# Moving POOL's four scatters of the routing table behind the mask of the next iteration, and cutting two of its subtractions into pieces

## The reference

```
x = x + xattn(layernorm(x), ctx, mask)
x = x + ffn(layernorm(x))

xattn: q = w8a8(x, wq, bq)            # rows and weights rounded to 8-bit integers
       k = ctx @ wk.T + bk            # ctx: 375 rows of 512 for each sequence, in float32
       v = ctx @ wv.T + bv
       attn = softmax(q k / sqrt(32) + mask)      # 16 heads of 32 channels
       return w8a8(attn v, wo, bo)
ffn:   probs = softmax(h @ router.T)              # 8 experts
       the two best experts of each token, their probabilities scaled to a sum of 1
       out = sum over both of p * (silu(gate) * up) @ down.T      # 352 inner channels
```

## Time and profile before

| What | Value |
|---|---|
| Median of 3 runs | 1654.12 us (1648.59 to 1658.02) |
| Profiled execution, its own time | 1643.64 us |
| Its span | 1641.9 us |
| Granted clock of PE, mean | 0.972 of full speed |
| PE busy | 1505.0 us, 92% of the span |
| DVE busy | 932.9 us, 57% |
| ACT busy | 880.2 us, 54% |
| POOL busy | 710.8 us, 43% |

### The profile page before, as it was taken

The page is one execution under the profiler, slowest core; times in us unless marked ns, Lnnn a source line. Parts: engine busy times, 40 slices in busy tenths (PEclk is TensorE's granted clock), DMA queues, the critical chain, the costliest instruction groups (busy, mean ns, idle before and its releaser), DMA issues. The chain is left out here.

```text
span 1641.9 us, 39981 instructions
## 1 busy us (share of the span) xinstructions
PE 1505.0 (92%) x11561; PEld 1319.5 (80%) x11562; DVE 932.9 (57%) x2531; ACT 880.2 (54%) x2112; POOL 710.8 (43%) x702
## 2 busy tenths in 40 slices
PE   2899999999999999999999999997199999999896
PEld 2788887888878888788887888886199999999895
DVE  6557776867768677686776867765322222222221
ACT  2466666666666666666666666665033333333232
POOL 4233435444354443544435444343345555555452
PEclk9899999999999999999999999997599999999998
DMA  5667776677766776667766677758236776765643
GB/s 197 170 173 207 196 203 180 175 215 178 208 173 179 210 196 190 173 182 206 197 189 173 182 209 189 196 148 267 68 62 163 171 172 143 167 148 115 167 77 46
DMA packets 219152, 281.53 MB, mean 171 GB/s; under 512 B 82081, under 2 KB 163873, under 8 KB 219105
## 3 DMA queue, kind: packets, MB, share of 16 engines
q1 hardware_dynamic: 200928, 247.78, 53.8%
q0 software_dynamic: 18176, 33.17, 11.5%
HBM read 118.12 MB, written 66.77 MB: 113 GB/s over the span
## 5 line engine op out<-in xcount | busy, mean ns | idle before, releaser
L503 ACT ACTIVATE probs<-probs,neg_max 112x375 f32<-112x375 f32 x512 | 311.8, 609 | 238.8 <-DVE neg_max L579 226.4
L579 DVE CUSTOM_DVE_ANT_0 probs<-score,neg_mask 112x375 f32<-112x375 f32 x512 | 279.5, 546 | 200.0 <-PE score L741 178.9
L749 PE MATMUL turn<-ident,probs 112*125 112x112 f32 x1536 | 265.1, 282 | 6.4 <-ACT probs L503 4.9
L749 PEld LDWEIGHTS turn<-ident,probs 112*125 112x125 f32 x1536 | 227.1, 191 | 40.5 <-issue 16.1
L496 ACT ACTIVATE probs_t<-turn 125x336 f32<-125x336 f32 x512 | 225.5, 440 | 56.4 <-PE turn L749 51.7
L741 PE MATMUL score<-k_stack,q_stack 96*112 96x376 f32 x512 | 209.4, 409 | 5.7 <-DMA q_stack<-q_lo 4.0
L777 PE MATMUL proj<-down_hi,gate_up_hi 128*128 128x376 f32 x512 | 175.6, 343 | 7.4 <-DVE gate_up_lo L606 5.7
L991 POOL DMA_INDIRECT out<-y_rows,entries x63 | 102.2, 1622 | 174.8 <-ACT y_rows L1017 138.8
L1029 DVE TENSOR_TENSOR a_lo<-a_ps,a_hi 128x384 fp32r<-128x384 f32 x63 | 35.1, 558 | 245.1 <-ACT a_hi L1004 157.1
L777 PE MATMUL proj<-down_lo,gate_up_hi 128*128 128x376 f32 x512 | 172.2, 336 | 0.0
L777 PE MATMUL proj<-down_hi,gate_up_lo 128*128 128x376 f32 x512 | 172.1, 336 | 0.0
(11 more groups left out here) (196 smaller groups left out, 3515.0 us busy)
## 6 DMA issues: line engine op xcount, KB each, us to landing
k_stack<-gate_up_hi SPq DMA_DIRECT2D x512, 94.0 KB, 2.2
k_stack<-gate_up_lo SPq DMA_DIRECT2D x256, 94.0 KB, 2.2
ctx_stage<-ctx_t SPq DMA_DIRECT2D x32, 750.0 KB
q_stack<-q_hi SPq DMA_DIRECT2D x256, 56.0 KB, 2.0
w_raw<-gate_up_t SPq DMA_DIRECT2D x32, 352.0 KB, 3.1
gate_up_dram_hi<-w_hi SPq DMA_DIRECT2D x32, 352.0 KB
gate_up_dram_lo<-w_raw SPq DMA_DIRECT2D x32, 352.0 KB
gate_up_hi<-gate_up_dram_hi SPq DMA_DIRECT2D x16, 704.0 KB
```

The source lines that it names most:

```text
L503: act.activation(probs[:, h % DS, :], probs[:, h % DS, :], ACT.Exp, bias=neg_max[:, par % 2, h:h + 1], scale=-1.0, accum_out=total[:, par ...
L579: dve.tensor_tensor_reduce(probs[:, h % DS, :], score[h % 2][0:N, 0:L], neg_mask[:, p, :], 1.0, BIG, ALU.add, ALU.min, neg_max[:, p, h:h + ...
L749: mm = pe.transpose(turn[h % 2][0:LC, l * N:(l + 1) * N], probs[:, h % DS, l * LC:(l + 1) * LC], W["ident"][0:N, 0:N])
```

## The change

The four scatters of a pair become a function of their own. It is called in the next even iteration, behind the negated mask L437 and ahead of the bias on q, and once more behind all iterations for the last pair. The two subtractions for the low parts are cut into instructions on one quarter of ctx (376 columns) and one third of the weights' slice (352 columns); the semaphore is raised by the last piece. Nothing that is computed changes.

```
+            def scatter(pair):
+
+                need(pool, weighing, WEIGH * pair + 6)
+                need(pool, routed, ROUTE * pair + 10)
+                waited(pool)
+                for b in range(2):
+                    for i in range(2):
+                        pool.indirect_dma_start(slots, bass.IndirectOffsetOnAxis(ap=at[:, b, i:i + 1], axis=0), entry[:, b, i, :], None).then_inc(entered, 16)
...
                     pool.tensor_scalar(neg_mask[:, q, :], neg_mask[:, q, :], -1.0, 0.0, ALU.mult, ALU.add).then_inc(mask_negated, 1)
+                if has_m2 and par % 2 == 0 and (inside or pair > 0):
+                    scatter(pair - 1)
                 if has_m2 and par % 2:
                     need(pool, top_made, 2 * pair + 2)
...
                     need(pool, c_hi_made, nn + 1)
-                    pool.tensor_tensor(c_lo[:, par % 2, :, :], stage[:, :, :], c_hi[:, par % 2, :, :].bitcast(F32),
-                                       ALU.subtract).then_inc(c_lo_made, 1)
+                    for t in range(KT):
+                        low = pool.tensor_tensor(c_lo[:, par % 2, t, :], stage[:, t, :], c_hi[:, par % 2, t, :].bitcast(F32), ALU.subtract)
+                    low.then_inc(c_lo_made, 1)
                 if has_n:
                     need(pool, w_hi_made, n + 1)
                     need(pool, w_stored, 64 * n)
-                    pool.tensor_tensor(w_lo[:, :], w_raw[:, :], w_hi[:, :].bitcast(F32), ALU.subtract).then_inc(w_lo_made, 1)
+                    for piece in range(3):
+                        cols = slice(piece * (WG + WD) // 3, (piece + 1) * (WG + WD) // 3)
+                        low = pool.tensor_tensor(w_lo[:, cols], w_raw[:, cols], w_hi[:, cols].bitcast(F32), ALU.subtract)
+                    low.then_inc(w_lo_made, 1)
...
-                    need(pool, weighing, WEIGH * pair + 6)
-                    need(pool, routed, ROUTE * pair + 10)
-                    waited(pool)
-                    for b in range(2):
-                        for i in range(2):
-                            pool.indirect_dma_start(slots, bass.IndirectOffsetOnAxis(ap=at[:, b, i:i + 1], axis=0), entry[:, b, i, :], None).then_inc(entered, 16)
 
             iterations(pool, body)
+            scatter(B // 2 - 1)
             pool.wait_ge(entered, 32 * B)
```

## The result

| | Before | Changed |
|---|---|---|
| Median, runs of the comparison | 1656.07 us (1648.59 to 1658.35, 4 runs) | 1691.2 us (1688.41 to 1696.95, 4 runs) |
| Ratio, 95% interval | | 1.0225 (1.0181 to 1.0269) |
| Profiled execution, own time | 1643.64 us | 1692.43 us |
| Its span, mean granted clock | 1641.9 us, 0.972 | 1690.7 us, 0.949 |

What follows compares the result with a forecast made beforehand. TensorE, busy 92% of the span, was taken as the bound. Ring +21.7, tail -1.5 and clock +18 gave +38 us on 1643.6, thus 1682, or 1692 us as median; range 1655 to 1716 us.

Steps and rivals of the forecast that it cites:

- The pause leaves L762: Product of probabilities and values, even iterations: TensorE's 2.27 us loss goes, its 48 matmuls taking 1.36 us.
- The ring grows by 1.55 us a pair: Loop q's split, SP's queue, mask, POOL, q's transpose, TensorE: mask-to-q 7.3 us against 5.74; +21.7 us over 14 pairs.
- rival 3: SP's queue and mask transfer quicken without scatters; mask 1.5 us earlier, ring unchanged, 1652 us; chance 0.10.
- 37.5 us or more: Sign: the way from q's transpose in the odd iteration to the even one, instead of 35.95 us.
- The clock falls in half of the fourteen: TensorE idling before q's transpose lowers its clock in half the even iterations, 2.6 us each: +18 us, ends 0 and 42.
- second rival: Wait for q comes and TensorE's clock falls in all fourteen even iterations: +56 us, 1710 us; chance 0.19.
- The pieces are worth 0: Cut subtractions on POOL: VectorE's L654 starts earlier, but the gain only lengthens idle time before L789; 0 us.
- The other end, -9 us: Best case for the cut subtractions, against the forecast of 0: a gain of 9 us.
- fifth rival: POOL takes the next piece before VectorE; L654 stays at 0.95 us. No time hangs on it; changes no chances.
- The tail, -1.5 us: Iteration 32, without q: of VectorE's 3.04 us wait for L427, about 1.5 us come back.
- I added 10.5 us: Step from profiled execution's forecast, 1682 us, to the median: the earlier runs' median, 1654.1, lay 10.5 us above that execution.

Runs made afterwards that it cites:

- TensorE kept busy: Changed kernel plus fourteen unread matmuls on TensorE ahead of its wait for q in even iterations: 1661.91 us, ratio 1.0061.
- the move alone: Changed kernel with the two subtractions whole again, scatters still moved: 1691.67 us, ratio 1.0236.
- early scatters and whole subtractions: Changed kernel with the scatters ahead of POOL's wait for the mask and both subtractions whole: 1657.22 us, ratio 1.0066.
- the last comparison: ACT's timelines in two changed kernels with scatters ahead of the mask's wait: mask also loaded ahead of keys' copies (1656.93 us) against without that (1619.36 us).
- 1641.87: Changed kernel with the mask's load issued ahead of the second half's keys' copies and both subtractions whole: 1641.87 us, ratio 0.9945.
- 1656.93: Changed kernel with pieces, mask's load ahead of the keys' copies and scatters ahead of the mask's wait: 1656.93 us, ratio 1.004.
- 1664.76: Kernel of 1657.22 us with ACT's and DVE's instructions shifted by 16 unused increments: 1664.76 us, ratio 1.0095.
- 1698.58: Changed kernel with the scatters one place later, behind the bias on q: 1698.58 us, ratio 1.03.
- 1612.1: Changed kernel, scatters and pieces kept, SP issuing the mask's load ahead of the second half's keys' copies: 1612.1 us, ratio 0.9747.
- 1619.36: Changed kernel, pieces kept, with the scatters moved ahead of POOL's wait for the mask: 1619.36 us, ratio 0.9795.

## Why the prediction was right, and where it was not

**The pause leaves L762: right.** The 48 matmuls take 1.36 us.

**The ring grows by 1.55 us a pair: right in its form, wrong in its size.** From the mask's negation to the transpose of q it takes 7.07 us on average, where 7.3 was worked out; the gap ahead of the first scatter is 0.41 us instead of 0.6. My mean for the kernel before, 5.74 us, is drawn down by the first even iteration; the thirteen others have 5.92. And one sentence failed: "Does the mask come earlier once TensorE is faster? It doesn't". The negation begins 25.09 us behind q's first copy instead of 25.67. Of these 0.58 us, 0.17 are SP's issuing and 0.41 the way from the load's issue to the negation. It is rival 3 with over a third of its size. So 7.07 - 5.92 - 0.58 = +0.57 us, and 0.55 were measured. The term was 7.2 + 3.1 = 10.3 us where 21.7 stood, below its own lower end of 17.5. The sign "37.5 us or more" was therefore missed: it was 36.48.

**The clock falls in half of the fourteen: the size right, the number wrong.** Behind a fall the way is 35.06 - 32.32 = 2.74 us longer, where 2.6 were taken; with TensorE kept busy 2.41 of these come back, and the other 0.33 stay without a cause shown. The fall came in thirteen of fourteen, thus 35.6 us instead of 18. Waits of 3.0 to 4.0 us (6.36 in the first) always brought it, and 1.71 us did not. My half was only a middle between a 3.42 us wait that lowered the clock and pauses of 2.27 us that never did; all new waits but one lay within 0.4 us of the former or above it, so the nearer row should have had nearly all the weight. It would be too much to read a limit into these numbers: in the kernel with the move alone 1.72 us were followed by a fall, and among waits of 1.3 to 2.3 us in the kernel with early scatters and whole subtractions five of thirteen were, without the longer ones being singled out.

The thirteen stretches at 0.56 to 0.63 are the loop that the Trainium skill describes in "TensorE: Matmul & The Clock Gate", section "HAM oscillation — how this bites in real kernels"; this trace agrees with it. The second rival was right about the clock, with a ring of half its size.

**The pieces are worth 0: right** in the changed kernel (1.0236 without, 1.0225 with them). The other end, -9 us, had the wrong sign in the kernel before, where they cost 0.6%, most of it in a longer pause. The fifth rival fell: L654's addition takes 499 ns instead of 951.

**The tail, -1.5 us**, can't be told from the 2.9 us that the span lost outside the pairs counted above.

**The sum.** +38 us were worked out, 48.8 came from span to span, and 35.1 between the medians of the comparison, since the profiled execution of before lay 12 us below that median. The two terms that were off went opposite ways, -11 and +18. That the forecast met the median within 1 us owes something to chance. I added 10.5 us because the profiled execution of before lay below its median; that of the changed kernel lies 1.2 us above its own.

## What to carry to other kernels

Before work is moved into a gap of an in-order queue, find what the gap waits for: here the gap was in front of the mask's wait, and work put just behind that wait is added to the ring that sets the pace. Price a new idle time of TensorE twice, once for itself and once for the clock behind it, and count on the fall where the wait is about as long as one that already brought it (3.0 us and more here, each time); shorter ones may bring it too. An engine's early release is worth nothing while a serial issue queue sets the date; moving one load ten microseconds up in that queue turned the changed kernel from 2.2% slower into 2.5% faster.

## What was not expected of the hardware

**Scatters hold other engines, in some kernels and not in others.** In the kernels with the hold TensorE, or ACT and DVE, stand still from about the third or fourth of POOL's four scatters on, and in most turns go on 0.9 to 1.7 us after the fourth has ended: 540.28 against 539.11 in the kernel before, 553.95 against 552.62 above. It comes in nearly all of the fourteen turns or in none. Where ACT and DVE stand, the signal they need is one of TensorE's, whose matmuls the records show as done; where it is TensorE, it stops within a product for which it waits for nobody. It belongs to the scatters and not to POOL's being busy. Shifts of ACT's and DVE's code by 16 instructions, and of TensorE's by 24, did not change it. Nor does the moment at which the scatters run decide it: in the last comparison it was the same against the other engines within 0.05 us, with the hold in one kernel and without it in the other.

With the hold are the kernels of 1641.87, 1656.93, 1657.22, 1664.76 and 1698.58 us and those with the old place of the scatters; without it those of 1612.1 and 1619.36 us, and for TensorE the one with the busy TensorE, whose fourteen matmuls run through the fourth scatter. The changed kernel and the move alone can't be put on either side: there TensorE has stopped for q before the fourth scatter begins (but for the last turn), and starts again 1.35 us after its end, so a hold would be hidden.

What makes the difference stays open. The pairs differ in SP's order, or in the length and timing of POOL's code. They also differ in the chip, and this was not tested: the kernels of 1612.1 and 1619.36 us ran on one chip, their siblings with the hold on two others, and none of these kernels on more than one. The kernel before took 1648 to 1652 us on all three, so the chips are alike for a kernel with the hold; for those without it nothing shows it. From sibling to sibling a pair with the hold is 2.1 to 3.5 us longer, falls of the clock included (68.30 against 66.16, 69.45 against 65.98). So a gain of 2.5% may be lost by an edit elsewhere, and must be measured again after each.

**A clock that falls costs no more after a long wait.** After 6.36 us of idle time, in one turn, the stretch read 0.58, as after 3.0 us (0.56).
